# The residual input of a gated layer: an accumulating DMA on the GpSimd queue, or a plain load on the SyncE queue and an add on VectorE

## The reference, cut to what matters

```python
x = L0_attn_X
xn = _layernorm(x)
s = xn + attention(xn)                 # 16 heads, 4 groups, softmax over 512 keys
g = silu(mixture_of_experts(xn))       # 64 experts, 8 for a token
x = x + s * g                          # x1: the place of the change
xn = _layernorm(x)
s = xn + alpha * state_space(xn)       # 512 channels x 16 states, scan over 512 tokens
g = silu(tree_ffn(xn))                 # 8 trees of depth 7
x = x + s * g
```

## Time and profile before

| | before |
|---|---|
| median of 3 runs | 3002.96 us |
| lowest, highest | 2997.28, 3013.54 us |
| profiled execution, its own time | 3002.96 us |
| its span, first to last instruction | 3001.2 us |
| granted TensorE clock, mean | 0.918 |
| busy: PE, DVE, ACT, POOL | 82%, 66%, 62%, 58% |

### The profile page before, as it was taken

How to read it: one execution, slowest core, us unless ns; L and a number is a source line. 1 busy time by engine, 2 the same in 40 slices (tenths; PEclk the granted TensorE clock), 3 DMA queues, 4 the chain that set the end, 5 groups by cost and what they waited for, 6 DMA issues and landing times.

```text
span 3001.2 us, 37634 instructions
## 1 busy us (share of the span) xinstructions
PE 2462.4 (82%) x12744; PEld 1387.2 (46%) x12744; DVE 1979.7 (66%) x2957; ACT 1852.0 (62%) x3346; POOL 1731.5 (58%) x1416
## 2 busy tenths in 40 slices
PE   5777679998689998998989898988898879866772
PEld 3444457764444454445444544454444544442331
DVE  4778744543366766776767677766767676778887
ACT  3456723346477785766667667775677667755752
POOL 1000054417657786777688759775876686544555
PEclk9888879999899999998989899999999989988896
DMA  4000158854545565545554455446544653366666
GB/s 142 22 18 5 49 167 236 242 174 69 94 116 108 109 142 130 113 99 111 135 113 100 108 129 110 85 95 141 114 86 94 133 110 81 85 134 138 158 158 144
DMA packets 281152, 344.83 MB, mean 115 GB/s; under 512 B 81600, under 2 KB 210510, under 8 KB 280960
## 3 DMA queue, kind: packets, MB, share of 16 engines
q0 software_dynamic: 84224, 176.19, 32.1%
q1 hardware_dynamic: 174224, 144.67, 16.6%
q10 hardware_dynamic: 22512, 21.57, 2.1%
HBM read 198.10 MB, written 26.80 MB: 75 GB/s over the span
## 4 chain that ended last, share of the span: by engine, by line
PE 44%; ACT 17%; issue 13%; DVE 13%; POOL 7%; DMA 4%; SPq 2%; another core or an unknown queue 0%; DVEq 0%; POOLq 0%; ACTq 0%
PE bank L1763 7%; PE bank L1752 6%; PE bank L1714 5%; PE bank L1899 4%; PE bank L1873 3%; PE bank L1928 3%; PE bank L1821 3%; DVE bank L1532 3%; ACT PT L1018 3%; POOL arena L1643 3%; PE bank L1775 3%; ACT Pr L998 2%; POOL acc_sb L1621 2%; DMA arena<-bc_dram 2%; PE bank L1998 2%
## 5 line engine op out<-in xcount | busy, mean ns | idle before, releaser
L1643 POOL TENSOR_TENSOR arena<-arena 128x512 f32<-128x512 f32 x512 | 859.8, 1738 | 169.7 <-DMA arena<-bc_dram 153.5
L1227 DVE TENSOR_REDUCE negmax<-bank 128x1 f32<-128x512 f32 x512 | 341.2, 681 | 258.7 <-PE bank L1752 257.8
L1621 POOL DMA_INDIRECT acc_sb<-ybuf,slot_idx x256 | 422.1, 1649 | 141.5 <-DMA ybuf<-arena 63.4
L1135 ACT ACTIVATE bank<-arena,A_sb 128x512 f32<-128x512 f32 x512 | 356.6, 699 | 223.5 <-DVE arena L1537 187.8
L1649 POOL TENSOR_TENSOR arena<-arena 128x512 f32<-128x512 f32 x192 | 279.0, 1453 | 323.5 <-DVE arena L1532 290.6
L1752 PE MATMUL bank<-Kp,Qp 64*128 64x512 f32 x1024 | 405.6, 683 | 70.5 <-ACT Pr L998 65.6
L1763 PE MATMUL bank<-ident,Pr 128*128 128x128 f32 x2048 | 353.4, 298 | 127.0 <-ACT PT L1018 63.8
L1532 DVE TENSOR_TENSOR_SCAN bank<-bank,arena 128x512 f32<-128x512 f32 x320 | 390.8, 1221 | 90.2 <-ACT bank L1135 53.3
L998 ACT ACTIVATE Pr<-bank,negmax 128x512 f32<-128x512 f32 x512 | 354.4, 692 | 154.8 <-DVE negmax L1227 138.4
L1018 ACT COPY PT<-bank 128x512 f32<-128x512 f32 x512 | 301.3, 588 | 204.9 <-PE bank L1763 189.9
L1763 PEld LDWEIGHTS bank<-ident,Pr 128*128 128x128 f32 x2048 | 228.9, 147 | 306.5 <-issue 106.3
(11 more groups left out here) (213 smaller groups left out, 3883.2 us busy)
## 6 DMA issues: line engine op xcount, KB each, us to landing
arena<-arena POOLq DMA_DIRECT2D x256, 512.0 KB, 5.4
arena<-bc_dram SPq DMA_DIRECT2D x256, 256.0 KB, 4.2
ybuf<-arena ACTq DMA_DIRECT2D x64, 256.0 KB
arena<-in_w_gate SPq DMA_DIRECT2D x64, 128.0 KB
arena<-in_w_up SPq DMA_DIRECT2D x64, 128.0 KB
arena<-in_w_down SPq DMA_DIRECT2D x64, 128.0 KB
arena<-in_X SPq DMA_DIRECT2D x8, 512.0 KB, 7.1
s_sb<-in_X SPq DMA_DIRECT2D x8, 512.0 KB, 9.1
```

The lines of the kernel that those rows point to most:

```text
L1135: act.activation(bank[DECAY[g % 2]][:, :], dt_sb[:, size_slot(b, cb), :], ACT.Exp, scale=A_sb[:, cb, n:n + 1]).then_inc(ssm_decay, 1)
L1227: dve.tensor_reduce(negmax[:, m % RING_STAT:m % RING_STAT + 1], bank[m % RING_S_ATT][:, :], AX.X, ALU.max, negate=True).then_inc(att_max, 1)
L1621: pool.indirect_dma_start(acc_sb[:, i, :], None, ybuf, bass.IndirectOffsetOnAxis(ap=slot_idx[:, b * TILES + i, k:k + 1], axis=0), bounds_c ...
L1643: pool.tensor_tensor(st_sb[:, g % RING_S, :], u_sb[:, size_slot(b, cb), :], B_sb[:, load % RING_BC, :], ALU.mult).then_inc(ssm_input, 1)
```

## The change

The sum x + s * g is made in another place. SP loads X[b] into x1 by one plain DMA of 512 KB at step 22 (for sequence 0 before the gathers). DVE multiplies acc_sb by s_sb in place and then adds acc_sb to x1, for each half. The two accumulating DMAs of POOL go. The waits for `stored` and `route_idx` move from DVE to SP. A semaphore cmb_x1 counts the adds; the clearing of acc_sb, the reload of s_sb and the statistics wait for it. silu moves from step 20 to 22, the multiplies (with the adds) from 22 and 23 to 24 and 25; statistics stay at 26. `inputs` has two pieces fewer, of which the loop for sequence 0 makes one `fill(FILL_PER_HEAD)` each.

```diff
-SILU_AT, HEAD_AT, LAST_AT, READY_AT = 20, 22, 60, 4
+LOAD_AT, HEAD_AT, LAST_AT, READY_AT = 22, 22, 60, 4
@@ inputs(b)
         for half in range(2):
             E.cmb_gate(b, half)
-            if half:
-                E.cmb_add(b, 0)
             yield 0
         done["gated"] = b + 1
-        E.cmb_add(b, 1)
-        for _ in range(2):
-            yield 0
         E.cmb_stats(b)
@@ beside(b, k, sides, ahead)
+            if k == LOAD_AT:
+                E.cmb_load(b + 1)
             if k == HEAD_AT:
                 fill_until("attention", b + 2)
                 fill_until("begun", b + 1)
                 gather_until(b + 2)
-            if k >= SILU_AT:
+            if k >= HEAD_AT:
                 next(ahead, 0)
@@ before the gathers of sequence 0
     E.cmb_begin(0)
+    E.cmb_load(0)
@@ SyncE
             def att_load(self, b):
                 if b >= 2:
-                    w.wait_ge(cmb_gate, 2 * (b - 1))
+                    w.wait_ge(cmb_x1, 2 * (b - 1))
+            def cmb_load(self, b):
+                w.wait_ge(stored[b % 2], 16 * (b // 2))
+                w.wait_ge(route_idx, PARTS)
+                sp.dma_start(x1[:, b % 2, :, :], X[b].rearrange("(t p) d -> p t d", p=P)).then_inc(x_cmb[b % 2], 16)
@@ VectorE
             def cmb_begin(self, b):
-                w.wait_ge(cmb_gate, 2 * b)
+                w.wait_ge(cmb_x1, 2 * b)
             def cmb_gate(self, b, half):
                 own = slice(TILES // 2 * half, TILES // 2 * (half + 1))
+                acc, x = whole(acc_sb[:, own]), whole(x1[:, b % 2, own])
                 w.wait_ge(cmb_silu, b + 1)
                 w.wait_ge(att_s, TILES * (b + 1))
-                w.wait_ge(stored[b % 2], 16 * (b // 2))
-                w.wait_ge(route_idx, PARTS)
-                dve.tensor_tensor(whole(x1[:, b % 2, own]), whole(acc_sb[:, own]), whole(s_sb[:, b % 2, own]), ALU.mult).then_inc(cmb_gate, 1)
+                dve.tensor_tensor(acc, acc, whole(s_sb[:, b % 2, own]), ALU.mult).then_inc(cmb_gate, 1)
+                w.wait_ge(cmb_gate, 2 * b + half + 1)
+                w.wait_ge(x_cmb[b % 2], 16 * (b // 2 + 1))
+                dve.tensor_tensor(x, x, acc, ALU.add).then_inc(cmb_x1, 1)
             def cmb_stats(self, b):
-                w.wait_ge(x_cmb[b % 2], 32 * (b // 2 + 1))
+                w.wait_ge(cmb_x1, 2 * (b + 1))
@@ GpSimd
-            def cmb_add(self, b, half):
-
-                own = slice(TILES // 2 * half, TILES // 2 * (half + 1))
-                w.wait_ge(cmb_gate, 2 * b + half + 1)
-                pool.dma_start(x1[:, b % 2, own, :], X[b].rearrange("(t p) d -> p t d", p=P)[:, own, :], accum_op=ALU.add).then_inc(x_cmb[b % 2], 16)
```

More of the change, by code:

```diff
@@ L93, in cmb_begin, with cmb_load @@
     def cmb_begin(self, b): pass
+    def cmb_load(self, b): pass
     def cmb_step(self, b, n): pass
@@ L96, in cmb_gate @@
     def cmb_gate(self, b, half): pass
-    def cmb_add(self, b, half): pass
     def cmb_stats(self, b): pass
@@ L665, in build_program @@
     x_cmb, gathered, stored = sems("x_cmb", 2), sems("gathered", TILES), sems("stored", 2)
-    cmb_zero, cmb_silu, cmb_gate, x1_norm = (sem(n) for n in ("cmb_zero", "cmb_silu", "cmb_gate", "x1_norm"))
+    cmb_zero, cmb_silu, cmb_gate, cmb_x1, x1_norm = (sem(n) for n in ("cmb_zero", "cmb_silu", "cmb_gate", "cmb_x1", "x1_norm"))
     tree_in_w, tree_out_w = sems("tree_in_w", RING_W), sems("tree_out_w", RING_W)
```

## The result

Measured in alternation with the kernel before, the changed kernel takes 3053.03 us (median of four, 3050.5 to 3055.25) against 3007.99 (2997.28 to 3013.54): a ratio of 1.0154, 95% interval 1.0119 to 1.0188, some 46 us (the two medians alone are 45 apart). That is outside my range (2978 to 3025) and on the side to which I gave 0.23. The profiled execution took 3042.99 us beside a span of 3041.2.

What follows compares the result with a forecast made beforehand. The prediction took a chain of hand-overs led by PE, with DVE not full, to bound the kernel. Its terms, -0.9 + 3.1 - 7.9 + 7.2 + 3.6 - 2.2, gave +2.9 on 3002.96: 3006 us, range 2978 to 3025.

Steps and rivals of the forecast that it cites:

- the side to which I gave 0.23: The outcome slower, against 0.52 for the same and 0.25 for faster; 0.5% or 15 us was the threshold.
- POOL's issues, -0.9: POOL loses sixteen DMA issues, 21.4 us, counting only where DVE waits for POOL's product: -0.9 us, bounds 0 and -21.4.
- The adds, +3.1: Sixteen new adds at the gates give DVE 6.3 us more work, half on the path: +3.1, bounds +1.6 and +20.3.
- Take half: Half of DVE's extra 6.3 us at the gates was counted, since DVE idles a third of the time, mostly for PE.
- Waits before the statistics, -7.9: DVE no longer waits for the accumulating DMA before the statistics, three waits: -7.9 us, bounds 0 and -7.9.
- Landing waits, +7.2: DVE's adds wait for SP's late load of x: 4 us at gate 4, 3.2 at gate 5; bounds 0 and +14.9.
- silu at gate 7, +3.6: silu, now behind the forced filling, delays a decay that DVE's scan needs at gate 7: +3.6 us; other gates 0.
- Start, -2.2: At gate 0 the statistics start earlier, at about 747 us, but filling left undone returns later: -2.2, bounds 0 and -4.5.
- The 2.4 units come back in the forced filling at batch 7: Attention work not done at gate 0 was to be made up in batch 7, offsetting part of the earlier start.
- The renamed waits, 0: Loading s_sb and clearing acc_sb wait on cmb_x1 in place of cmb_gate, tens of steps later or on DVE itself: 0.
- The third rival: DVE's adds are caught by POOL: +20.3 for +3.1, 3023 us; decides at 15 us more gate time, all awaited; chance 0.10.
- My closing warning: The shift of filling against scan steps would mislead the sum most, changing which weight load SP stands at all through.

Runs made afterwards that it cites:

- e8: e4 with DVE's 16 additions left out, so x is missing from the result but still loaded and waited for; 2987.2 us, ratio 0.9934.
- e4: The changed kernel with the load of x at step 18, all gate pieces at their old steps and both empty pieces back; 2984.66 us, ratio 0.9959.
- e6: The changed kernel with the load of x at step 18 and two empty pieces put back for sequence 0 alone; 3021.51 us, ratio 1.0053.
- e5: e4 with the mark that releases clearing and gathers set at step 26 in place of 24; 3010.52 us, ratio 1.0015.
- e9: e4 with two gathers more, at scan steps 26 and 28, so the last stands two steps earlier; 3010.73 us, ratio 1.0021.

## Why the prediction was wrong

The steps by their numbers.

1. *POOL's issues, -0.9:* within its bounds, sized too small. DVE's waits for POOL's product are 49.0 us after (30.0 + 19.0) against 49.1, as forecast, and yet without the adds the exchange was worth 0.66% (20 us, e8), of which steps 1 and 3 account for 8.8. The view that I trusted, who waits for POOL, does not show what POOL costs DVE: lengthened DVE instructions count as busy. The sixteen multiplications of the kernel before hold 9.4 us of such excess, (1.269 - 0.683) x 16; in e8, at 740 ns on average, about one is left. The issues do not hold DVE themselves, so if they cost it time, it was by where they put POOL's products; that is argued, not tried. How the rest divides between issues and waits was not tried, and of the 20 us the trace of e8 shows 9.4 from the first scan on.

2. *The adds, +3.1:* 33.5 us of work against the 26.7 that I gave, +13.2 in place of +6.3; in e4 28.9, near my price. "Take half" agrees with e8 over e4 (7.5 of 14.8 us, but 10 us either way). With half, the term should have been some 7.

3. *Waits before the statistics, -7.9:* they are gone, as said; their worth alone was not measured.

4. *Landing waits, +7.2:* right mechanism, right gates, size off. 8.22 and 8.35 us, 16.6 in all, just above my upper bound of 14.9; moving the load gave back 14 to 20. At gate 5 SP did pass the load ahead of the out weights, as the shift had it, but it had come late to the step, from out weights that held it 6.03 us from 2097.51: SP's own waits moved with everything else. I took a lateness of the old trace as a constant.

5. *silu at gate 7, +3.6:* the wait behind it measured 3.63. But "at seven gates both places lie in running work: 0" failed: silu and gates two steps later cost 11 us, in gate multiplications and adds caught beside POOL's products (10.1 us more of DVE's time in e6 than in e5).

6. *Start, -2.2:* the statistics of gate 0 stand at 743.11 against 751.56, further than my bound, but 3.3 us of that were there at the first gather (675.5 against 678.8), and the first scan starts 3.3 us earlier as well (818.1 against 821.4). So the start gained nothing by this trace. "The 2.4 units come back in the forced filling at batch 7" is what failed: the lag is carried through seven batches and costs 10 to 21 us.

7. *The renamed waits, 0 ("clearing acc_sb" among them):* here the largest term is missing. I looked at the renamed semaphore, which costs nothing, and not at done["gated"], which moved from step 24 to 26 and took the clearing and 32 gathers a batch with it: 17 us by the runs, 8.2 by the traces (e5 over e4). I counted what the moved pieces do themselves, and not what their mark releases.

So the failed steps are 7 (a term left out), the second halves of 5 and 6, and the size of 4. The third rival named the right physics, a DVE instruction caught by POOL's products, and saw a part of the places: the gates cost DVE 13.2 us more, near its condition of 15, but the largest excess came in the multiplication by g, 13.6 us more, which the change doesn't touch. The rule of the Trainium skill (SBUF — State Buffer, Who interferes with whom), that a VectorE instruction with two SBUF inputs contends with a GpSimd one that reads SBUF, agrees with each of them: fin by g and acc_sb by s_sb both read two SBUF tiles. What my use of it missed is the size: the 4.78 us of the earlier trace rows were already more than one instruction of POOL, whose products there took 2.07 and 2.06 us. That the removed DMA issues are not what held the multiplies was right. My closing warning named the shift of filling as what would mislead the sum most; it cost about as much as the mark, and had no term in the sum beyond SP's order.

What stays open: where e4's gain lies, and whether the mechanism or the earlier load brings it; why the kernel before stands in a good phase, beyond that in the traces both the lag and the lead lengthen fin by g (15.1 and 15.0 us above its quick instances, 7.0 before), and the lag the xs products as well (28.7 against 21.4); how much of e4's gain is POOL's and how much the waits'; and what part the clock has. PE's 12744 matmuls took 2473.6 us after and 2462.4 before, at a granted clock of 0.915 and 0.918 in the profiled executions, and slower executions of one kernel mostly show a lower clock; no experiment parts cause from consequence there.

## What to carry to other kernels

When a schedule is written out by hand and has been fitted, split a change into its mechanism and its displacement and time both: here by the runs the mechanism gained 12 us, and its placing, the load's step and the lag included, lost 58. Follow every mark that a moved piece sets to the generators that wait for it, not only its semaphores. And a load put into a queue that blocks elsewhere is issued when the queue gets there; put it ahead by the stands of that queue seen in the trace and the landing (here 5.74 and 6.03 us, and a landing of about 9), not by its landing time alone.

## What the hardware showed that I had not expected

A DVE instruction with two SBUF inputs is held until one of POOL's tensor_tensors ends, and not always the first: 0.42 us became 5.63, and 0.68 became 5.63, each beside several products of POOL with a DMA issue among them. All 35 long ones of the two traces end 0.29 to 1.09 us, by their size, after such an end; 320 multiplications with one input in PSUM took 690 to 693 ns throughout. What decides how many products it is held over, one to four, stays open. The waits and the share of busy time hide this, since the time counts as DVE's own. And what an issue on POOL costs depended on its step more than on its 1.65 us: two steps later, with the clearing (e5), the gathers cost 17 us, two a batch brought forward (e9) 19.
